# A four-layer graph network on one core: the transposes between layers 2 and 3 at other places in TensorE's order, and two operations on ScalarE in place of VectorE

## The reference

```python
# layer 2: attention, softmax over masked scores, then elu
attention = jax.nn.softmax(scores, axis=1)
x = x + jax.nn.elu(attention @ Wh)
h = jnp.maximum(_layernorm(x, axis=-1), 0.0)
# layer 3, with h as points x: for every pair (i, j) of nodes with adj > 0
u = _mobius_add(-x, y)                  # needs only |x|^2, |y|^2 and x.y
un = clip(norm(u)); log = 2.0 / _lambda_x(x) * arctanh(un) * (u / un)
v = sum over j of the masked logs; result = _expmap(v, x)
```

## Time and profile before

| what | value |
|---|---|
| time, median of 3 runs | 975.49 us (974.43 to 976.28) |
| profiled execution: its own time | 974.21 us |
| profiled execution: span of the trace | 972.2 us |
| TensorE busy, over the span | 893.5 us (92%) |
| VectorE busy | 712.9 us (73%) |
| ScalarE busy | 556.9 us (57%) |
| GpSimd busy | 533.9 us (55%) |
| mean granted TensorE clock | 0.927 of full speed |

### The profile page before, as it was taken

One profiled execution on the slowest core, in us unless ns is written; L12 is line 12 of the kernel. 1 busy time (PEld: TensorE's weight loads), 2 busy tenths in 40 slices (PEclk: granted clock), 3 DMA queues, 4 the chain that ended last, 5 costly groups with the idle time before them and its releaser, 6 DMA issues.

```text
span 972.2 us, 18079 instructions
## 1 busy us (share of the span) xinstructions
PE 893.5 (92%) x7000; PEld 333.3 (34%) x7000; DVE 712.9 (73%) x1190; ACT 556.9 (57%) x995; POOL 533.9 (55%) x660
## 2 busy tenths in 40 slices
PE   6899999999999999999999799999979887899981
PEld 6733222222222222222222532333333335555650
DVE  4655557887878877887878678411559778999986
ACT  2689657666656656666656487100130165788853
POOL 3367659889898888988887010000000034688841
PEclk9679999999999999999999879999969866999986
DMA  8671211121212102111000000000000000000000
GB/s 171 155 133 38 56 59 40 31 69 36 74 33 69 37 23 75 41 60 42 27 14 23 2 1 1 1 2 1 1 1 1 1 0 0 1 1 1 1 1 22
DMA packets 23036, 32.65 MB, mean 34 GB/s; under 512 B 14587, under 2 KB 14715, under 8 KB 21926
## 3 DMA queue, kind: packets, MB, share of 16 engines
q1 hardware_dynamic: 20646, 23.11, 8.4%
q0 software_dynamic: 2304, 8.39, 4.7%
HBM read 38.58 MB, written 1.29 MB: 41 GB/s over the span
## 4 chain that ended last, share of the span: by engine, by line
PE 74%; DVE 17%; issue 4%; ACT 3%; DMA 0%; POOL 0%; DVEq 0%; ACTq 0%
PE ps L1486 23%; PE ps L1496 11%; PE ps L1670 9%; PE ps L1473 6%; DVE big L499 5%; PE ps L1465 4%; PE ps L1618 3%; PE ps L1739 2%; PE ps L1728 2%; PE ps L1342 2%; DVE big L932 2%; DVE big L496 2%; PE ps L1453 1%; DVE big L637 1%; PE ps L1749 1%
## 5 line engine op out<-in xcount | busy, mean ns | idle before, releaser
L637 DVE COPY_PREDICATED big<-mask,ps 128x512 f32<-128x512 uint8 x512 | 341.7, 729 | 113.9 <-PE ps L1473 109.4
L447 POOL TENSOR_SCALAR big<-big 128x512 f32<-128x512 f32 x512 | 356.7, 713 | 77.0 <-PE ps L1496 74.8
L1124 ACT ACTIVATE ps<-ps 128x512 f32<-128x512 f32 x512 | 268.8, 583 | 146.3 <-PE ps L1465 146.0
L1486 PE MATMUL ps<-big 128*32 128x512 f32 x2048 | 254.7, 602 | 0.0
L473 POOL TENSOR_TENSOR big<-big 128x512 f32<-128x512 f32 x34 | 56.3, 1657 | 262.3 <-ACT big L1269 262.3
L1496 PE MATMUL ps<-big 128*32 128x512 f32 x1024 | 135.4, 601 | 0.0
L1465 PE MATMUL ps<-op_r,op_l 18*128 18x512 bf16 x512 | 112.5, 385 | 5.5 <-DVE big L637 3.8
L1486 PEld LDWEIGHTS ps<-big 128*32 128x32 f32 x2048 | 53.7, 109 | 120.1 <-issue 109.8
L1473 PE MATMUL ps<-op_r,op_l 9*128 9x512 bf16 x512 | 74.9, 389 | 0.8 <-ACT ps L1124 0.5
L1728 PE MATMUL ps<-big 66*128 66x512 f32 (+3 forms) x160 | 73.5, 595 | 2.1 <-DVE big L496 2.1
L1473 PEld LDWEIGHTS ps<-op_r,op_l 9*128 9x128 bf16 x512 | 18.2, 91 | 154.5 <-ACT ps L1124 108.8
(11 more groups left out here) (308 smaller groups left out, 1109.2 us busy)
## 6 DMA issues: line engine op xcount, KB each, us to landing
big<-max_scratch SPq DMA_DIRECT2D x8, 1024.0 KB, 4.9
big<-rden_scratch SPq DMA_DIRECT2D x30, 256.0 KB, 3.3
big<-in_adj_dram POOLq DMA_DIRECT2D x12, 512.0 KB, 9.7
op_l<-split_scratch SPq DMA_DIRECT2D x56, 36.0 KB
op_r<-split_scratch SPq DMA_DIRECT2D x56, 36.0 KB
work<-in_adj_dram POOLq DMA_DIRECT2D x2, 512.0 KB, 13.5
h_nat<-in_adj_dram POOLq DMA_DIRECT2D x2, 512.0 KB, 11.9
x_nat<-in_x_dram SPq DMA_DIRECT2D x1, 512.0 KB, 4.8
```

What stands on the lines that cost most here:

```text
L447: pool.tensor_scalar(ring[:, k % RING, :], vrow[:, head % 2, i0:i0 + HALF], HUGE, g0[:, head, jt:jt + 1], ALU.min, ALU.max).then_inc(s["ba ...
L637: dve.copy_predicated(ring[:, k % RING, :], mask[:, jt, i0:i0 + HALF], ps[:, slot("tile", k), :])\
L1124: act.activation(ps[:, at_slot, :], ps[:, at_slot, :], ACT.Relu, scale=-1.0).then_inc(s["relus"], 1)
L1486: m = pe.matmul(ps[32 * w:32 * (w + 1), MAIN, :], vp[:, head, jt + w // 2, 32 * (w % 2):32 * (w % 2 + 1)], ring[:, (u + w // 2) % RING, :] ...
```

## The change

- `turn_out(0)` moves on TensorE from behind pair 2 of layer 2's second half to behind pair 0.
- `turn_left(0)` moves from behind pair 6 to ahead of it; `turn_right(0)` stays behind pair 6.
- `turn_left(1)` moves from behind TensorE's step 4 of layer 3 to behind step 5.
- The Relu that makes `h` from the centred values goes from VectorE (L859) to ScalarE, ahead of its first square, in both halves.
- `rden` of half 1 goes from VectorE (`scaled_part(1)`) to ScalarE, which reads the transposes in PSUM right after it has copied `lhs3`. That of half 0 stays on VectorE. `turn_right(1)`, which overwrites those banks, now waits for it.

```diff
@@ center_part(b) on VectorE
                 dve.scalar_tensor_tensor(work[:, of, :], wide(stat[:, 0, of]), -1.0 / D, x[:, of, :], ALU.mult, ALU.add)\
                     .then_inc(s["part_in"], 1)
-                dve.wait_ge(s["part_in"], 3 * b + 2)
-                ts(h[:, of, 0:D], work[:, of, :], 0.0, None, ALU.max).then_inc(s["part_in"], 1)
@@ scaled_part on VectorE
-            def scaled_part(b):
-                dve.wait_ge(s["g_read_b"], 2 * b + 1)
-                ts(rden[0:DX, b * TW:(b + 1) * TW], lhs3[0:DX, b * TW:(b + 1) * TW], minus2, None, ALU.mult).then_inc(s["g_read"], 1)
+            def scaled_part():
+                dve.wait_ge(s["g_read_b"], 1)
+                ts(rden[0:DX, 0:TW], lhs3[0:DX, 0:TW], minus2, None, ALU.mult).then_inc(s["g_read"], 1)
...
-                elif k == 6:
-                    scaled_part(1)
@@ squares_part(b) on ScalarE
-                act.wait_ge(s["part_in"], 3 * b + 2)
+                act.wait_ge(s["part_in"], 2 * b + 2)
+                act.activation(h[:, of, 0:D], work[:, of, :], ACT.Relu).then_inc(s["relus"], 1)
                 act.activation(elu[:, of, :], work[:, of, :], ACT.Square).then_inc(s["part_out"], 1)
-                act.wait_ge(s["part_in"], 3 * b + 3)
+                act.wait_ge(s["relus"], TILES0 + BLOCKS + b + 1)
                 act.activation(relu2[:, of, :], h[:, of, 0:D], ACT.Square).then_inc(s["part_out"], 1)
@@ left_part(b) on ScalarE
+                if b == 1:
+                    act.activation(rden[0:DX, TW:2 * TW], ps[0:DX, 6:8, :].rearrange("p b n -> p (b n)"), ACT.Copy, scale=minus2)\
+                        .then_inc(s["g_read"], 1)
@@ turn_right(b) on TensorE
                 if b == 1:
-                    pe.wait_ge(s["g_read_b"], 3)
+                    pe.wait_ge(s["g_read"], 2)
@@ layer 2's pairs on TensorE
                 for jp in range(NT // 2):
+                    if b == 1 and jp == NT // 2 - 2:
+                        turn_left(0)
                     pe.wait_ge(s["gated"], b * NT + 2 * jp + 2)
...
-                    if b == 1 and jp == 2:
+                    if b == 1 and jp == 0:
                         turn_out(0)
                     if b == 1 and jp == NT // 2 - 2:
-                        turn_left(0)
                         turn_right(0)
@@ layer 3's steps on TensorE
                 if k == 1:
                     turn_out(1)
-                elif k == 4:
+                elif k == 5:
                     turn_left(1)
                 elif k == 6:
                     turn_right(1)
```

More of the change, by code:

```diff
@@ L846, in activate @@
                     .then_inc(s["part_in"], 1)
-                dve.wait_ge(s["part_in"], 3 * b + 1)
+                dve.wait_ge(s["part_in"], 2 * b + 1)
                 link(dve.scalar_tensor_tensor(x[:, of, :], work[:, of, :], 0.0, x[:, of, :], ALU.max, ALU.add))
@@ L904, in _ @@
                         .then_inc(s["gated"], 1)
-            scaled_part(0)
+            scaled_part()
             top2 = (1.0 - 1e-5) ** 2
@@ L1217, in exp_part @@
             def exp_part(b):
-                act.wait_ge(s["part_in"], 3 * b + 1)
+                act.wait_ge(s["part_in"], 2 * b + 1)
                 act.activation(elu[:, rows_of(b), :], work[:, rows_of(b), :], ACT.Exp).then_inc(s["part_out"], 1)
```

## The result

The changed kernel took 962.93 us (median of 4 runs, 961.85 to 965.32), the kernel before 974.96 in the same comparison. The ratio is 0.9881, interval 0.9855 to 0.9908. By the ratio it is 11.6 us.

A forecast was written before the change was run, and what follows sets the result against it. VectorE and TensorE were both taken as full in steady layer 3, so the gain lay in VectorE's waits for TensorE at the joint before it: 6.0 + 0.5 + 2.1 = 8.6 us, forecast 967.0 us, range 963.5 to 971.0.

The forecast's parts named there:

- part 1: Layer 2's second half: earlier `turn_out(0)` and `turn_left(0)` start `distances(0)` at 773.1 instead of 779.09, 6.0 us; low bound 3.1.
- part 2: Half 1 in layer 3: 0.5 us from the Relu leaving VectorE and 2.1 us from moving `turn_left(1)`.
- I take the full clock: Layer 2, behind `turn_out(0)`: dense pairs follow, so TensorE keeps full clock; half clock would cost 1.6 or 2.9 us.
- The new wait of tile 8: Layer 2, second half: VectorE waits some 0.55 us for denominators behind pair 1, as `turn_out(0)` runs ahead of them.
- The first rival: Layer 2: the clock falls behind the earlier `turn_out(0)`; total gain 5.7 to 7.0, 968.5 to 969.8 us; chance 0.22.
- The order's term: Layer 3: with `turn_left(1)` later, tile 5's wait of 3.26 us goes and TensorE's chain to tile 7 shortens, 2.1 us.
- The term of 0.5 us for the Relu: Layer 3, half 1: Relu of 1.53 us leaves VectorE, but its wait for GpSimd moves to L926; 0.5 us saved.
- the further meetings: Layer 3: two more VectorE meetings with GpSimd before `norm_part(1)` ends, a reason to take only 0.5 us saved.
- The scaled operand: Layer 3: `scaled_part(1)` leaves VectorE with no separate gain; ScalarE's copy costs 1.00 us, with 2 to 3 us of cover.
- Early rise: Layer 3: clock rises right after `turn_left(1)`, VectorE's two steps then bound; total gain 10.8, 964.7 us; chance 0.10.
- Slower: Layer 3: TensorE's low clock lasts beyond tile 7, each further tile costing 3.7 us; 978 us; chance 0.03.
- nothing changed: Both VectorE waits return elsewhere, at tile 8 and through ScalarE's copies holding up `turn_right(1)`; 975 us; chance 0.03.

The follow-up runs named there:

- The two further comparisons: The changed kernel run twice more without any edit, against the kernel before: 966.29 us, ratio 0.9918, and 966.09 us, ratio 0.9912.
- the order for half 0 only: The kernel before with only `turn_out(0)` behind pair 0 and `turn_left(0)` ahead of pair 6: 970.75 us, ratio 0.9968.
- the order alone: The kernel before with only `turn_left(1)` moved from behind step 4 to behind step 5: 966.78 us, ratio 0.9938.
- 34 added transposes: The changed kernel with 34 useless identity transposes in TensorE's waits of layer 3's steps 3 to 5, run twice: 961.96 and 961.74 us.
- 22 added transposes: The changed kernel with 22 useless identity transposes in TensorE's waits of layer 3's steps 3 to 5: 963.83 us, ratio 0.9915.

## Why the prediction was right or wrong

**The sum came close, the range was too narrow.** The worked sum was 8.6 us. The two further comparisons gave 8.0 and 8.6; from the join to the end the three profiles of the changed kernel gave 7.6, 9.4 and 11.0 (in the third, 1.6 us of it lie behind tile 7, far behind the change). Part of the closeness is luck: part 1 gave 0.4 to 2.1 us less than forecast and part 2 gave 0.9 more, as told below. The step that failed is the one from the sum to the range: it took in the unknown costs of the change, but counted the 740 us ahead of it at nothing. The join moved over 9 us in 16 profiles of the same code, and a median of four runs keeps part of that. In the first pair of profiles 4.6 of the 12.2 us between the spans are that lead. Another 0.5 us is the starting point: the forecast took 975.49 us for the kernel before, and the comparison measured 974.96. Nothing in the first comparison's four times alone shows how much of the 12.0 us is the lead; the profile does for its one execution, and the later comparisons make it likely for the others. That it was chance there too is inferred, not shown; an early rise of the clock in layer 3, as in two later profiles, is not ruled out for the three executions that have no profile.

**Part 1, forecast 6.0 us.** Measured 5.6 where the clock stayed up (33.24 - 27.64) and 3.9 where it fell. The step "I take the full clock" failed in the first profile. The new wait of tile 8, forecast at 0.55, was 0.79 and 2.48. The first rival had its mechanism right and its price too: a gain of 3.1 to 4.4 was worked out for it. `turn_out(0)` was followed by a fall in four of the ten profiles that have it behind pair 0 (31.31 and 29.3 us from join to tile 0, against 27.6 to 28.1 in the others), and in all six that have it behind pair 1 or 2; the 0.22 given to it looks low, though ten profiles are few. The four with a fall have their join at 741.12 to 746.73 us, the six without at 746.41 to 750.28. So a short lead and a fall mostly came together, and in the first comparison's profile the fall took back 1.7 of the 4.6 us that the lead gave; whether one brings the other is not shown. The Trainium skill (TensorE: Matmul & The Clock Gate, part 1) makes the clock follow how busy TensorE has been. The profile's busy time does not show that here: TensorE was busy in every microsecond from 740 to 752, and the clock still stood at 0.50 from 748 to 751, in an order of work that kept it at 1.00 in six other profiles.

**Part 2, forecast 2.6 us.** Measured 3.5 at tile 7 (42.99 - 39.5). The stall of 3.26 us went as forecast, and a wait of 2.67 us came for tile 7, forecast at some 3. The order's term, forecast 2.1, is 14.3 - 12.1 = 2.2 us. The term of 0.5 us for the Relu was mis-sized: `norm_part(1)` ends 1.3 us earlier behind tile 0 (808.86 - 780.18 = 28.7 before, 799.09 - 771.70 = 27.4 now), and tile 4 stands 1.3 us earlier than with the Relu put back on VectorE. The wait for GpSimd did move on to L924 (1.32 us instead of 0.68), but only that once; the further meetings that I deducted for cost nothing extra. So the Relu's place itself gave 1.45 - 0.64 = 0.8 us. The other 0.5 is a wait of 0.46 us at tile 1's distance, which stands in all five profiles with the Relu on VectorE and in none of the eleven with it on ScalarE; why is not shown. Tile 4 also moves with the clock: with the order for half 0 only it stood at 19.94 us with the Relu still on VectorE, and the clock fell 8.5 us behind tile 0 there, 6 in the kernel before. The Trainium skill (SBUF — State Buffer, the two separate sides) has the one of VectorE and GpSimd that starts second wait until the other's operation ends. The rows agree: L924 started 0.50 us behind GpSimd's operation, took 0.64 us longer than alone, and ended 0.55 us after it. By single edits the split at tile 7 is another: the order alone gave 3.1 us, and as much when taken back, and ScalarE's two operations on top of it only 0.4 (39.87 to 39.5), since the clock rose 37 us behind tile 0 with them and without.

**The scaled operand** was worth nothing at tile 7, as forecast: 39.46 us with it and without it. ScalarE's copies delayed `turn_right(1)` only in the two profiles with 34 added transposes, by 0.86 and 0.87 us.

**Early rise, forecast 4.8 us for all of part 2.** Seen once without added work: 36.18 us, 6.8 less than before. Tile 7 started 9.6 us behind `norm_part(1)` (812.36, after its last operation at 802.55 + 0.17), at the forecast bound of about 10; the rest of the difference is that `norm_part(1)` itself ended 2.1 us earlier behind tile 0, not 0.5.

**Slower, and nothing changed:** neither was seen. The long low stretch ended before tile 7 in every profile. A second, short one began some 11 us behind tile 7 in both profiles of the kernel before (0.50 from 834 to 837 us in the first) and in five others, in none of the three of the changed kernel; it cost little: from tile 7 to the end the kernel before took 149.0 us and the changed one 148.8 in its first two profiles.

**What was named as a sign:** the wait at L843 gone, a wait at tile 8 (longer than "under 1 us" in the first profile), no wait at tile 5, 2.67 at tile 7, all there. `distances(0)`, forecast near 773, began at 770.5, 774.9 and 772.9 us in the three profiles, and the clock was up again at about 809, 813 and 811, forecast 812 to 815. The clock of 0.50 right behind `turn_out(0)`, named as a sign against the forecast, was there too in the first profile.

## What to carry to other kernels

A change near the end of a long program is measured through everything ahead of it: mark the last instruction that both versions share, and compare from there, or widen the range by how far that mark moves. Moving sparse transposes out of the way of a waiting engine pays in full only if TensorE's clock holds, so look at what it does right behind them. Where TensorE waits at low clock just before dense work, useless work in the wait can be worth more than an operation taken off the busiest engine: here 2.8 us against 0.4 at tile 7, both from profiles; the whole times show the first only weakly.

## What the runs showed of the hardware that was not expected

- The same code up to the first join took from 741.12 to 750.28 us in 16 profiles.
- In kernels with the same order on TensorE in layer 3 the clock rose about 31, 33 or 37 us behind tile 0, and tile 7 started at 36.2, 38.2 or 39.5 us.
- With 22 added transposes the clock rose at about 794.6 us and fell again at about 804.9, in a wait of 4.07 us; with 34 it held through a wait of 2.77.
- The clock stood at 0.50 in the middle of a stretch in which TensorE was never idle (740 to 752 us in the changed kernel's first profile).
